# Closing layer norm of layer 1: beta joins the kept rows in the projections' stage, ACT normalises, and the gate's matmul has stationary weights

## The chip, the core and the metric

The kernel runs on one core of a Trainium2 chip. The metric is the time of the whole program on the device, in microseconds (us); lower is better. The engines named here are PE (TensorE), DVE (VectorE), ACT (ScalarE), POOL (GpSimd), and SP (SyncE), which issues most DMAs. Each runs its own list of instructions in order and waits for others on semaphores.

## The reference, cut to what matters

Four sequences of 1024 tokens (4096 rows of width 256) go through two layers. Layer 0 is windowed attention and a mixture of experts; layer 1 is full attention in groups, a layer norm with residual, and experts whose tokens are chosen with a Sinkhorn normalised gate. Only these lines bear on the change:

```python
# layer 1: attention on the normalised rows, _layernorm(x) is the block's input
out = ctx @ wo + bo
out = out + x                                   # x: the normalised input rows
mu, var = mean(out), var(out)
out = (out - mu) * rsqrt(var + 1e-5) * gamma + beta
# outer residual, then the next block's input norm and gate
x = x_before + out
y = _layernorm(x)                               # "routed rows"
gate_logits = einsum("bnd,de->bne", y, gate_w)  # 8 experts
```

So each row of `x_before` is needed again after attention, with `beta` added to it, and each new row is normalised once more, stored, and multiplied by a 256 x 8 gate.

## The kernel before, in words

The 4096 rows lie in SBUF as 32 tiles of 128 rows, `g.x[:, t, :]`, with `g.mean` and `g.rstd` beside them. Layer 1's first half is `attention1`, four stages one after the other with a barrier between them: `project_groups`, `group_attention`, `finish_stats`, `norm_residual`. Two of them are touched by the diff.

**Projections' stage (`project_groups`, names `pg_`).** There are 16 pairs of tiles, in 8 rounds of two (s = 0, 1). In a round DVE normalises 4 tiles into `pg_xn` (L1510), PE transposes them (L1579), ACT copies them out (L1546), PE makes queries and keys (L1590) and values (L1598), ACT writes the rounded part `pg_hi` (L1555), DVE the rest `pg_lo` (L1520) and the values `pg_v` (L1525), and SP stores all of it to DRAM. Beside this, x itself must be kept in DRAM and then be replaced in SBUF by `xn + bo`: SP stores the pair of tiles straight out of `g.x` (`keep_x`, L1434), POOL waits until that store has landed and adds `bo` (L1485). Between its first rounds POOL also sets six pieces of the key stack `a_ks` to one (L1493), two after each of the adds of rounds 0, 2 and 4. All is ordered by hand: DVE's loop is `rests(r, 0)`, `normalise(r + 1)`, `rests(r, 1)`; PE's is project, four transposes for each of two pairs, project; SP's is `keep(r, 0)`, `keep_x(r + 1)`, `keep(r, 1)`, and in rounds 1 to 4 six loads for the attention (L1382). `pg_hi` and `pg_lo` have one buffer for each s, so ACT and DVE may write those of round r + 1 only when the stores of round r have landed (`parts_out`).

**Closing stage (`norm_residual`, names `nr_`).** Eight steps of four tiles. SP loads gamma, beta, the kept rows `nr_xb` in four quarters and the gate. POOL adds beta to `nr_xb` (L1975, eight instructions of 128 x 1024). For each step DVE makes `(x - mean) * gamma` (L1986), then the new x (L1992), its statistics (L1997) and seven small operations (L2001 to L2011); ACT takes the root (L2036); DVE inverts it (L2015) and normalises the four tiles of the step before into `nr_xn` (L2021). SP stores these rows, PE transposes them (L2062), ACT copies them (L2042), PE multiplies with the transposed tile as the stationary operand and the 8 columns of the gate moving (L2068), and ACT copies the logits out (L2045). After the barrier comes `sinkhorn`, which needs all logits.

Of the kernel before, what the change touches and what calls it, by code (L numbers as in the profile page):

```python
# [1389 lines left out]
def project_groups(nc, g, parts, values, x_kept, qs, ks, v):  # L1390
# [4 lines left out]
    with phase(nc) as (e, semaphore, begin):  # L1395
# [13 lines left out]
        xn_ready, xnT_done, xnT_ready, qk_done, hi_ready, lo_ready, v_done, v_ready, xn_bo_ready = [sem(n) for n in (  # L1409
            "xn_ready", "xnT_done", "xnT_ready", "qk_done", "hi_ready", "lo_ready", "v_done", "v_ready", "xn_bo_ready")]  # L1410
# [4 lines left out]
        W_IN, B_IN, PARTS = 16 * 3, 16 * (2 * KD + A + 1), 16 * 4  # L1415

        @block.sync
        def _(sp):
# [8 lines left out]
            sp.dma_start(bo[:], ins["L1_attn_bo"].rearrange("(o n) -> o n", o=1).broadcast_to([P, D])).then_inc(b_in, 16)  # L1427
# [43 lines left out]
        def _(pool):  # L1471
# [5 lines left out]
            pool.wait_ge(b_in, ONE + B_IN)  # L1477

            def residual(r):
                for s in range(2):  # L1480
                    i = 2 * r + s
                    pool.wait_ge(x_out[s], ONE + 16 * r + 16)
                    for h in range(2):
                        pool.wait_ge(xn_ready, ONE + 2 * i + h + 1)
                        nc.gpsimd.tensor_tensor(g.x[:, bass.ds(2 * i + h, 1), :].rearrange("p o d -> p (o d)"),  # L1485
                                                xn[s][h][:], bo[:], ALU.add).then_inc(xn_bo_ready, 1)

            for a in range(SLOTS):
                residual(2 * a)
                pool.wait_ge(xn_bo_ready, ONE + 4 * (2 * a + 1))  # L1490
# [3 lines left out]
                pool.wait_ge(k_ones, ONE + 2 * (a + 1))  # L1494
                residual(2 * a + 1)
            with pool.Fori(2 * SLOTS, STEPS) as r:
                residual(r)

        @block.vector
        def _(dve):  # L1500
# [12 lines left out]

            def rests(r, s):
# [410 lines left out]
def norm_residual(nc, g, x_kept, gate, logits, rows_out):  # L1925
# [3 lines left out]
    C = 4  # L1929
    STEPS = T // C  # L1930
    QUARTERS = 4
    with phase(nc) as (e, semaphore, begin):
        sb = lambda n, shape, dt=F32: e.enter_context(nc.sbuf_tensor(f"nr_{n}", shape, dt))
        sem = lambda n: semaphore(f"nr_{n}")
        gamma, beta, eps = sb("gamma", [P, D]), sb("beta", [P, D]), sb("eps", [P, 1])
        xb = sb("xb", [P, T, D])
        gw = sb("gw", [P, KD, E])
        scaled = sb("scaled", [P, C, D])
        diff, var = sb("diff", [P, C]), sb("var", [P, C])
        xn = [sb(f"xn{s}", [P, D]) for s in range(C)]  # L1940
        xnT = [sb(f"xnT{s}", [P, KD, P]) for s in range(C)]
        w_in, gate_in, xb_ready, scaled_ready, x_ready, stats_ready, step, var_ready, std_ready, rstd_ready = [sem(n) for n in (
            "w_in", "gate_in", "xb_ready", "scaled_ready", "x_ready", "stats_ready", "step", "var_ready", "std_ready", "rstd_ready")]
        xn_ready, xnT_done, xnT_ready, l_done, l_ready = [sem(n) for n in (
            "xn_ready", "xnT_done", "xnT_ready", "l_done", "l_ready")]
        xb_in = [sem(f"xb_in{n}") for n in range(QUARTERS)]
        rows_kept = [sem(f"rows_kept{s}") for s in range(C)]
        block = begin()
        b_tp, b_l = g.bank[0:C], g.bank[C]
        four = lambda i: bass.ds(C * i, C)  # L1950

        @block.sync
        def _(sp):
# [453 lines left out]
```

## Time and profile before

| what | us |
|---|---|
| time, median of 3 runs | 2563.13 |
| lowest and highest of the 3 | 2553.75, 2564.44 |
| the profiled execution's own time | 2581.78 |
| its span in the trace | 2579.9 |
| PE, DVE, ACT, POOL busy | 2096.3, 1623.0, 1009.0, 453.7 |

The busy times are sums over the whole program; each stage has a bound of its own. The projections' stage lies at about 1338 to 1468 us of the span and the closing stage at about 2241 to 2338 us. How far a time in the trace is from the start of the span is what the first column of a timeline shows.

### The profile page before, as it was taken

Reading aid. Unit: us, or ns where it says so; the run is one execution under the profiler, and the core shown is the slowest. Engines: PE = TensorE matmul, PEld = TensorE weight load, DVE = VectorE, ACT = ScalarE, POOL = GpSimd, SP = SyncE. Lnnn points to the kernel's source line nnn. Section 1 sums busy time; section 2 is a strip of 40 time slices with the busy share of each in tenths; the row PEclk is TensorE's granted clock in tenths of the full one; section 3 lists DMA queues with packets and bytes.
Section 4 is the critical chain, followed back from the end, with each engine's and each line's share of the span. In section 5 each row is a group of like instructions: output and inputs, shape, how many; then the busy total and the mean of one; then the engine's idle time right before and its main releaser. Section 6 shows DMA issues by size and latency. Waiting matters only on the chain. (4 is left out here: it accounts for less than half of the span.)

```text
span 2579.9 us, 47888 instructions
## 1 busy us (share of the span) xinstructions
PE 2096.3 (81%) x16968; PEld 1310.4 (51%) x16969; DVE 1623.0 (63%) x2749; ACT 1009.0 (39%) x1885; POOL 453.7 (18%) x612
## 2 busy tenths in 40 slices
PE   2888888679799999996968899999999999643150
PEld 2666666368566666665857633333333333242140
DVE  4666666557443334334654599999999999286922
ACT  2545554332100000002322257777877778410010
POOL 3000000200111111102434111111111111110054
PEclk9999999889899999997989879999999999855585
DMA  2000000551211111113328888755754700210054
GB/s 82 2 0 0 0 0 0 196 221 66 79 41 41 41 41 41 41 37 126 110 73 272 230 60 71 60 46 46 64 37 41 61 2 2 70 49 16 1 162 131
DMA packets 207090, 171.36 MB, mean 66 GB/s; under 512 B 121772, under 2 KB 184920, under 8 KB 204920
## 3 DMA queue, kind: packets, MB, share of 16 engines
q1 hardware_dynamic: 186872, 126.57, 26.2%
q0 software_dynamic: 17792, 26.39, 3.8%
q10 hardware_dynamic: 2304, 16.78, 1.8%
q8 instruction: 76, 1.25, 0.2%
q14 instruction: 46, 0.38, 0.1%
HBM read 105.43 MB, written 63.97 MB: 66 GB/s over the span
## 5 line engine op out<-in xcount | busy, mean ns | idle before, releaser
L1760 DVE TENSOR_REDUCE ga_nmax<-banks 128x1 fp32r<-128x1024 f32 x512 | 620.7, 1220 | 47.1 <-PE banks L1836 45.5
L1791 ACT ACTIVATE ga_probT<-banks 128x512 f32<-128x512 f32 x1024 | 553.4, 598 | 180.3 <-PE banks L1849 133.8
L1836 PE MATMUL banks<-a_ks,a_qs 48*128 48x512 f32 x1024 | 378.6, 457 | 28.1 <-DVE ga_nmax L1760 22.8
L1849 PE MATMUL banks<-a_qs,a_ks 49*128 49x512 f32 x1024 | 375.6, 447 | 0.7 <-ACT ga_probT L1791 0.7
L1865 PE MATMUL banks<-ga_probT,a_v 128*32 128x256 f32 (+1 forms) x3840 | 320.4, 406 | 6.4 <-ACT ga_o L1797 6.4
L1836 PEld LDWEIGHTS banks<-a_ks,a_qs 48*128 48x128 f32 x1024 | 159.4, 193 | 238.1 <-DVE ga_nmax L1760 174.4
L1275 PE MATMUL banks<-m_w,rb_xT 128*128 x576 | 273.8, 598 | 0.0
L1748 POOL DMA_DIRECT2D a_qs<-ga_max_rows x256 | 130.8, 519 | 599.7 <-DVE ga_max_rows L1767 556.4
L1257 ACT ACTIVATE rb_silu<-banks 128x512 f32<-128x512 f32 x72 | 43.0, 597 | 435.0 <-PE banks L1275 435.0
L1088 PE MATMUL banks<-sh_xnT,sh_w 128*128 128x512 f32 x768 | 184.9, 399 | 32.0 <-DVE sh_w L874 30.9
L1088 PEld LDWEIGHTS banks<-sh_xnT,sh_w 128*128 128x128 f32 x768 | 146.4, 193 | 65.1 <-issue 34.9
L1849 PEld LDWEIGHTS banks<-a_qs,a_ks 49*128 49x128 f32 x1024 | 154.5, 186 | 24.8 <-ACT ga_probT L1791 21.8
L1865 PEld LDWEIGHTS banks<-ga_probT,a_v 128*32 128x32 f32 x3840 | 76.0, 108 | 179.1 <-ACT ga_probT L1791 129.5
L1275 PEld LDWEIGHTS banks<-m_w,rb_xT 128*128 128x128 f32 x576 | 110.3, 191 | 78.1 <-issue 70.6
L346 DVE TENSOR_REDUCE wa_nmax<-banks 128x4 f32<-128x512 f32 x128 | 87.0, 680 | 95.3 <-PE banks L543 95.3
L1195 POOL DMA_INDIRECT rb_xb<-normalised_rows,m_source x72 | 68.4, 950 | 385.9 <-PE banks L1268 385.4
L1302 PE MATMUL banks<-rb_w,rb_gluT 128*128 x576 | 135.9, 378 | 0.0
L414 ACT ACTIVATE wa_probT<-banks 128x512 f32<-128x512 f32 x128 | 76.4, 597 | 128.9 <-PE banks L555 128.9
L1228 DVE TENSOR_SCALAR rb_own_out<-rb_row_e,m_block_f 128x128 fp32r<-128x128 f32 x72 | 20.7, 287 | 151.1 <-PE banks L1292 151.1
L1302 PEld LDWEIGHTS banks<-rb_w,rb_gluT 128*128 128x128 f32 x576 | 104.1, 190 | 11.6 <-issue 0.2
L555 PE MATMUL banks<-ident,wa_prob 128*128 128x128 f32 x512 | 85.8, 291 | 25.7 <-ACT wa_prob L407 25.7
L407 ACT ACTIVATE wa_prob<-wa_ex 128x512 f32<-128x512 f32 x128 | 80.5, 629 | 51.9 <-DVE wa_ex L348 51.0
(297 smaller groups left out, 3256.6 us busy)
## 6 DMA issues: line engine op xcount, KB each, us to landing
sh_xnT<-xnT_parts ACTq DMA_DIRECT2D x16, 1024.0 KB, 4.9
sorted_out<-rb_yb SPq DMA_DIRECT2D x72, 128.0 KB, 1.7
xnT_parts<-np_parts SPq DMA_DIRECT2D x8, 1024.0 KB, 7.7
m_w<-in_L_ffn_rw_dram SPq DMA_DIRECT2D x2, 4096.0 KB
values<-pg_v SPq DMA_DIRECT2D x16, 512.0 KB, 3.1
a_v<-values SPq DMA_DIRECT2D x16, 512.0 KB, 9.0
a_qs<-queries_rounded SPq DMA_DIRECT2D x28, 256.0 KB, 8.8
a_ks<-keys_rounded SPq DMA_DIRECT2D x28, 256.0 KB, 10.1
```

The source lines that it names most:

```text
L346: nc.vector.tensor_reduce(nmax[k][:], sc, axis=AX.X, op=ALU.max, negate=True).then_inc(max_ready, 1)
L407: nc.scalar.activation(prob[k][:], ex[k][:], ACT.Exp, scale=SCALE).then_inc(prob_ready, 1)
L555: last = nc.tensor.transpose(b_pt[k][:, P * j:P * (j + 1)], prob[k][:, j, :], g.ident[:])
L1088: last = nc.tensor.matmul(bank[m % 2][:], w[a][:, k, P * m:P * (m + 1)], xnT[s][:, b, k, :], start=(k == 0 and a + b == 0), stop=(k == KD ...
L1275: last = nc.tensor.matmul(bank[:], xT[s][:, k, :], flat[:, bass.ds(n * KD + k, 1), :].rearrange("p o h -> p (o h)"), start=False, stop=(k ...
L1302: last = nc.tensor.matmul(b_y[:, 0:D], gluT[:, m, :], flat[:, bass.ds(n * KH + m, 1), :].rearrange("p o d -> p (o d)"), start=False, stop= ...
L1748: nc.gpsimd.dma_start(dst, src).then_inc(max_in[1][b % 2], 16)
L1760: nc.vector.tensor_reduce(nmax[b % 2][:, at:at + 1], slot[:], axis=AX.X, op=ALU.max, negate=True).then_inc(use_read, 1)
L1791: nc.scalar.activation(probT[k % SETS][2 * h + n][:], b_t[ring_place["weights", w] % RING][:], ACT.Exp, scale=SCALE).then_inc(exp_ready, 1)
L1836: return nc.tensor.matmul(slot[:, HALF * kh:HALF * (kh + 1)], qs[a][rows, n, P * q:P * (q + 1)], ks[a][rows, n, HALF * kh:HALF * (kh + 1)] ...
L1849: nc.tensor.matmul(bank[:], ks[a][rows, 2 * gp + n, P * kt:P * (kt + 1)], qs[a][rows, 2 * gp + n, HALF * hf:HALF * (hf + 1)], start=True, ...
L1865: last = nc.tensor.matmul(b_o[at:at + BL, cols], v[c % SLOTS][:, h, 2 * gp + n, kt, :], probT[k % SETS][2 * h + n][:, cols], start=(kt == ...
```

## The change

In the projections' stage beta is loaded too. DVE now writes `x + beta` of each pair into a new buffer `pg_kept` (one for each s), SP stores from that buffer, and DVE, not POOL, adds `bo`. These two are a new function `residual(r + 1)` at the end of DVE's loop body. `keep_x` waits for `kept_ready`. POOL has only its memsets left and no longer waits for adds between them.

In the closing stage the loop over steps is unrolled. POOL has no adds; it sets the gate's 128 x 256 tile to zero once. DVE no longer normalises; it stores the negated mean, and ACT normalises in two passes, `x + (-mean)` and then times `rstd`. The gate's weights, padded with zeros to 128 columns, are now the stationary operand, and 512 tokens move; the 128 x 512 result is copied by ACT (`nr_lT`), turned back by four transposes on PE, and then copied to the logits. PE and ACT work one and two steps behind the rows.

```diff
@@ project_groups
+        beta = sb("beta", [P, D])
+        kept = [sb(f"kept{s}", [P, 2, D]) for s in range(2)]
...
             def keep_x(r):
                 for s in range(2):
                     i = 2 * r + s
-                    sp.wait_ge(xn_bo_ready, ONE + 4 * r)
-                    sp.dma_start(x_dst[bass.ds(i, 1)].rearrange("i p s d -> (i p) s d"), g.x[:, bass.ds(2 * i, 2), :]).then_inc(x_out[s], 16)
+                    sp.wait_ge(kept_ready, ONE + i + 1)
+                    sp.dma_start(x_dst[bass.ds(i, 1)].rearrange("i p s d -> (i p) s d"), kept[s][:]).then_inc(x_out[s], 16)
...
@@ gpsimd
-            pool.wait_ge(b_in, ONE + B_IN)
...
+            pool.wait_ge(v_one, ONE + 2)
             for a in range(SLOTS):
-                residual(2 * a)
-                pool.wait_ge(xn_bo_ready, ONE + 4 * (2 * a + 1))
+                if a:
+                    pool.wait_ge(k_ones, ONE + 2 * a)
                 for h in range(2):
                     rows = slice(HR * h + BL, HR * h + HR)
                     nc.gpsimd.memset(ks[a][rows].bitcast(F32), 1.0).then_inc(k_ones, 1)
-                pool.wait_ge(k_ones, ONE + 2 * (a + 1))
-                residual(2 * a + 1)
-            with pool.Fori(2 * SLOTS, STEPS) as r:
-                residual(r)
@@ vector
+            def residual(r):
+                for s in range(2):
+                    i = 2 * r + s
+                    pair = g.x[:, bass.ds(2 * i, 2), :]
+                    dve.wait_ge(x_out[s], ONE + 16 * r)
+                    nc.vector.tensor_tensor(kept[s][:], pair, beta[:].unsqueeze(1).broadcast_to([P, 2, D]),
+                                            ALU.add).then_inc(kept_ready, 1)
+                    dve.wait_ge(kept_ready, ONE + i + 1)
+                    dve.wait_ge(xn_ready, ONE + 2 * i + 2)
+                    for h in range(2):
+                        nc.vector.tensor_tensor(g.x[:, bass.ds(2 * i + h, 1), :].rearrange("p o d -> p (o d)"),
+                                                xn[s][h][:], bo[:], ALU.add).then_inc(xn_bo_ready, 1)
...
             normalise(0)
+            residual(0)
             with dve.Fori(0, STEPS - 1) as r:
                 rests(r, 0)
                 normalise(r + 1)
                 rests(r, 1)
+                residual(r + 1)
@@ norm_residual, vector
             def inverse(i):
                 dve.wait_ge(std_ready, ONE + i + 1)
                 nc.vector.reciprocal(g.rstd[:, four(i)], g.rstd[:, four(i)]).then_inc(rstd_ready, 1)
-                dve.wait_ge(rstd_ready, ONE + i + 1)
...
-                    nc.vector.tensor_scalar(xn[s][:], tile(g.x, t), g.mean[:, bass.ds(t, 1)], g.rstd[:, bass.ds(t, 1)],
-                                            ALU.subtract, ALU.mult).then_inc(xn_ready, 1)
...
             new_x(0)
-            with dve.Fori(1, STEPS) as i:
+            for i in range(1, STEPS):
                 new_x(i)
-                normalise(i - 1)
-            normalise(STEPS - 1)
+                inverse(i - 1)
+            inverse(STEPS - 1)
@@ norm_residual, scalar
+                for c in range(C):
+                    t = C * i + c
+                    nc.scalar.activation(xn[i % 2][:, c, :], g.x[:, t, :], ACT.Identity,
+                                         bias=g.mean[:, t:t + 1]).then_inc(centred_ready, 1)
+                act.wait_ge(rstd_ready, ONE + i + 1)
+                for c in range(C):
+                    t = C * i + c
+                    act.wait_ge(centred_ready, ONE + t + 1)
+                    nc.scalar.activation(xn[i % 2][:, c, :], xn[i % 2][:, c, :], ACT.Copy,
+                                         scale=g.rstd[:, t:t + 1]).then_inc(xn_ready, 1)
...
+            for i in range(STEPS + 3):
+                if i < STEPS:
+                    root(i)
+                    normalised(i)
+                if 1 <= i <= STEPS:
+                    transposed(i - 1)
+                if 2 <= i <= STEPS + 1:
+                    gated(i - 2)
+                if i >= 3:
+                    kept(i - 3)
@@ norm_residual, tensor
+                for k in range(KD):
+                    last = nc.tensor.matmul(b_g[i % 2], gw[:, k, :], xnT[i % 2][:, k, :], start=(k == 0), stop=(k == KD - 1))
+                last.then_inc(gate_done, 1)
...
+            for i in range(STEPS + 2):
+                if i < STEPS:
+                    transposes(i)
+                if 1 <= i <= STEPS:
+                    gates(i - 1)
+                if i >= 2:
+                    turned(i - 2)
```

Three places in the order of instructions matter. The first is POOL's whole list in the projections' stage. Before, it was this (the names are those above; `ISA` and the like are waits and loop code):

```order
L1473 MEMSET pg_v 128x1024 x2
L1476 MEMSET pg_v 128x32 x2
L1485 TENSOR_TENSOR x<-pg_xn,pg_bo 128x256 x4
L1493 MEMSET a_ks 32x4096 x2
L1485 TENSOR_TENSOR x<-pg_xn,pg_bo 128x256 x8
L1493 MEMSET a_ks 32x4096 x2
L1485 TENSOR_TENSOR x<-pg_xn,pg_bo 128x256 x8
L1493 MEMSET a_ks 32x4096 x2
L1485 TENSOR_TENSOR x<-pg_xn,pg_bo 128x256 x4
```

Now it is this, with the barrier's and the stage's branch ahead of it and the jump behind:

```order
L77 UNCONDITIONAL_BRANCH
L1473 UNCONDITIONAL_BRANCH
L1476 MEMSET pg_v 128x1024 x2
L1479 MEMSET pg_v 128x32 x2
L1486 MEMSET a_ks 32x4096 x6
L64 UNCONDITIONAL_BRANCH
```

The adds are gone, and the six memsets of the key stack, which stood in three places, follow each other at the stage's start.

The second place is DVE at the start of the same stage, with the first part of its loop. Before:

```order
L1510 TENSOR_SCALAR pg_xn<-x,mean,rstd 128x256 x4
L1529 UNCONDITIONAL_BRANCH
L1529 ISA
L1519 ISA
L1520 SCALAR_TENSOR_TENSOR pg_lo<-banks,pg_b_qk,pg_hi 128x256 x2
```

And now:

```order
L1499 TENSOR_SCALAR pg_xn<-x,mean,rstd 128x256 x4
L1508 TENSOR_TENSOR pg_kept<-x,pg_beta 128x512
L1513 TENSOR_TENSOR x<-pg_xn,pg_bo 128x256 x2
L1508 TENSOR_TENSOR pg_kept<-x,pg_beta 128x512
L1513 TENSOR_TENSOR x<-pg_xn,pg_bo 128x256 x2
L1532 UNCONDITIONAL_BRANCH
L1532 ISA
L1521 ISA
L1522 SCALAR_TENSOR_TENSOR pg_lo<-banks,pg_b_qk,pg_hi 128x256 x2
```

Six additions stand between the last normalised tile and the first `pg_lo`; the same six stand at the end of each of the loop's seven turns.

The third place is the end of the closing stage on PE. There it ended with one more turn of the same loop, four times two transposes and 16 small products. Now its last rows are these, where `nr_xn` is transposed at L2089, the gate is applied at L2097 and the logits are turned at L2105:

```order
L2089 MATMUL banks<-ident,nr_xn 128x128 x8
L2097 MATMUL banks<-nr_xnT,nr_gw 128x512 x2
L2105 MATMUL banks<-ident,nr_lT 128x128 x4
L2097 MATMUL banks<-nr_xnT,nr_gw 128x512 x2
L2105 MATMUL banks<-ident,nr_lT 128x128 x8
```

Behind the last rows' transposes there are now two gates and twelve turning transposes, where one step's products stood before.

## Rows read from the trace of the kernel before

**Rows 1.** Timeline, closing stage's opening: start us, us, engine line op out<-in xcount [idle before <-releaser]

```profile
2249.97 19.14 POOL L1975 TENSOR_TENSOR nr_xb<-nr_xb,nr_beta 128x1024 f32 x8 [50.66 <-DMA nr_xb<-x_kept]
2252.34 9.98 DVE L1992 SCALAR_TENSOR_TENSOR x<-nr_scaled,rstd,nr_xb 128x256 f32<-128x256 f32 x4 [4.58 <-POOL nr_xb L1975]
```

**Rows 2.** Timeline, closing stage, a steady step and the end

```profile
2278.04 1.67 DVE L1986 SCALAR_TENSOR_TENSOR nr_scaled<-x,mean,nr_gamma 128x256 f32<-128x256 f32 x4
...
2281.68 1.41 DVE L1997 BATCH_NORM_STATS2 stats<-x  x4 [0.16 <-DVE x L1992]
...
2284.34 0.18 DVE L2015 RECIPROCAL rstd<-rstd  x1
...
2284.89 1.38 DVE L2021 TENSOR_SCALAR nr_xn<-x,mean,rstd 128x256 f32 x4 [0.37 <-DVE rstd L2015]
...
2286.32 1.67 DVE L1986 SCALAR_TENSOR_TENSOR nr_scaled<-x,mean,nr_gamma 128x256 f32<-128x256 f32 x4
...
2325.57 0.16 DVE L2011 TENSOR_SCALAR rstd<-nr_var 128x4 f32 x1
...
2326.81 1.96 PE L2062 MATMUL banks<-ident,nr_xn 128*128 128x128 f32 x8 [3.10 <-DVE nr_xn L2021]
...
2337.04 0.20 ACT L2045 ACTIVATE gate_logits<-banks 128x32 f32<-128x32 f32 x1 [2.83 <-PE banks L2068]
```

**Rows 3.** Stretches: us, busy (x) of PE, PEld, DVE, ACT, POOL, PEclk, DMA share, GB/s

```profile
2300.00:2330.00 30.00, 18.73 (x88) 18.46 (x88) 25.19 (x87) 7.91 (x23) 0.00 (x0) 0.50 0.20 70
```

**Rows 4.** Timeline, opening of the projections' stage

```profile
1340.36 0.21 POOL L1476 MEMSET pg_v<- 128x32 f32 x2
...
1343.33 0.62 SPq L1427 DMA_DIRECT2D pg_bo<-in_L_attn_bo_dram  x1
...
1346.81 1.80 DVE L1510 TENSOR_SCALAR pg_xn<-x,mean,rstd 128x256 f32<-128x256 f32 x4 [9.77 <-DMA pg_bo<-in_L_attn_bo_dram]
...
1349.57 2.81 PE L1590 MATMUL banks<-pg_xnT,pg_wq 128*128 128x256 f32 x8
...
1356.81 1.98 DVE L1510 TENSOR_SCALAR pg_xn<-x,mean,rstd 128x256 f32 x4
```

**Rows 5.** Timeline, later rounds of the projections' stage

```profile
1372.68 1.37 DVE L1510 TENSOR_SCALAR pg_xn<-x,mean,rstd 128x256 f32 x4
...
1383.19 0.88 DVE L1520 SCALAR_TENSOR_TENSOR pg_lo<-banks,pg_b_qk,pg_hi 128x256 fp32r<-128x256 f32 x2 [2.29 <-ACT pg_hi L1555]
...
1387.54 1.96 SPq L1434 DMA_DIRECT2D x_kept<-x  x2
...
1390.37 0.84 ACT L1555 ACTIVATE pg_hi<-banks,pg_b_qk 128x256 fp32r<-128x256 f32 x2 [1.71 <-PE banks L1590]
...
1408.73 7.06 POOL L1493 MEMSET a_ks<- 32x4096 f32 x2
...
1414.19 2.72 DVE L1510 TENSOR_SCALAR pg_xn<-x,mean,rstd 128x256 f32 x4
...
1430.75 1.37 DVE L1510 TENSOR_SCALAR pg_xn<-x,mean,rstd 128x256 f32 x4
```

**Rows 6.** Instructions on pg_xn: engine op xcount: ns min/median/max, starts, forms

```profile
L1510 DVE TENSOR_SCALAR pg_xn<-x,mean,rstd x32: 394/407/1760, 1346.8 to 1445.6; 128x256 f32 x28, 128x256 f32<-128x256 f32 x4
```

**Rows 7.** DMA issues, 1380 to 1405 us: KB each, median us to landing

```profile
keys_rest<-pg_lo SPq DMA_DIRECT2D x4, 256.0 KB, 3.0
```

**Rows 8.** Timeline, layer 0's stage with the gate in the same form

```profile
487.03 1.09 ACT L669 ACTIVATE np_xnT<-banks 128x512 f32<-128x512 f32 x2
...
487.32 1.88 PE L720 MATMUL banks<-np_xnT,np_gw 128*128 128x512 f32 x4
...
489.04 0.60 PE L728 MATMUL banks<-ident,np_lT 128*128 128x128 f32 x4
```

**Rows 9.** Groups by line and shape, ACT: busy us, mean ns, idle before

```profile
L1042 ACT ACTIVATE sh_p<-sh_p 128x256 f32<-128x256 f32 x1 | 0.4, 416 | 0.0
```

**Rows 10.** Groups by line, PE, 689 to 704 us

```profile
L1275 PE MATMUL banks<-m_w,rb_xT 128*128 x15 | 10.4, 832 | 0.0
```

More of the change, by code:

```diff
@@ L1942, in norm_residual @@
[L1942 to L1945, printed above, removed]
+        xn = [sb(f"xn{u}", [P, C, D]) for u in range(2)]
+        xnT = [sb(f"xnT{u}", [P, KD, C * P]) for u in range(2)]
@@ L1946, in norm_residual @@
         xb_in = [sem(f"xb_in{n}") for n in range(QUARTERS)]
-        rows_kept = [sem(f"rows_kept{s}") for s in range(C)]
+        rows_kept = [sem(f"rows_kept{u}") for u in range(2)]
         block = begin()
-        b_tp, b_l = g.bank[0:C], g.bank[C]
-        four = lambda i: bass.ds(C * i, C)
+        b_tp = [g.bank[2 * u:2 * u + 2] for u in range(2)]
+        b_g, b_l = g.bank[4:6], g.bank[6:8]
+        four = lambda i: slice(C * i, C * (i + 1))
+        half = lambda h: slice(TH * P * h, TH * P * (h + 1))
@@ L2048, in _, with normalised @@
-            root(0)
-            with act.Fori(1, STEPS) as i:
-                root(i)
-                transposed(i - 1)
-            transposed(STEPS - 1)
+            def normalised(i):
+                if i >= 2:
+                    act.wait_ge(xnT_done, ONE + HALVES * (i - 1))
+                    act.wait_ge(rows_kept[i % 2], ONE + 16 * (i // 2))
+                for c in range(C):
[8 more added lines that the diff above has]
+                                         scale=g.rstd[:, t:t + 1]).then_inc(xn_ready, 1)
@@ new lines, in transposed @@
+            def transposed(i):
+                for h in range(HALVES):
+                    act.wait_ge(xnT_done, ONE + HALVES * i + h + 1)
+                    if i >= 2 and h == 0:
+                        act.wait_ge(gate_done, ONE + i - 1)
+                    dst = xnT[i % 2][:, :, half(h)].rearrange("p k (t q) -> p t k q", t=TH)
+                    nc.scalar.activation(dst, b_tp[i % 2][h].rearrange("p (t k q) -> p t k q", t=TH, k=KD),
+                                         ACT.Copy).then_inc(xnT_ready, 1)
@@ new lines, in gated, with kept @@
+            def gated(i):
+                act.wait_ge(gate_done, ONE + i + 1)
+                if i >= 2:
+                    act.wait_ge(l_done, ONE + i - 1)
+                nc.scalar.activation(lT[i % 2][:], b_g[i % 2], ACT.Copy).then_inc(lT_ready, 1)
+            def kept(i):
+                act.wait_ge(l_done, ONE + i + 1)
+                src = b_l[i % 2].rearrange("p (c q) -> p c q", c=C)[:, :, 0:E]
+                nc.scalar.activation(logits[:, four(i), :], src, ACT.Copy).then_inc(l_ready, 1)
@@ new lines, in transposes @@
+            def transposes(i):
+                for h in range(HALVES):
+                    if i >= 2:
+                        pe.wait_ge(xnT_ready, ONE + HALVES * (i - 2) + h + 1)
+                    for c in range(TH):
+                        t = TH * h + c
+                        pe.wait_ge(xn_ready, ONE + C * i + t + 1)
+                        for k in range(KD):
+                            at = P * (KD * c + k)
+                            last = nc.tensor.transpose(b_tp[i % 2][h][:, at:at + P], xn[i % 2][:, t, P * k:P * (k + 1)], g.ident[:])
+                    last.then_inc(xnT_done, 1)
```

117 lines of the change are left out of this document (49 added, 68 removed).

## The prediction, made before the changed kernel ran

> **What bounds the kernel now.** I began with the page's busy times only to see that no engine is busy throughout, so each stage is read by itself. The timeline of the closing stage came next, because most of the change is there. Its opening shows DVE waiting for POOL: POOL starts its eight additions when the first quarter of the kept rows is in, at 2249.97, and holds on for 19.14 us; DVE's first four additions to x, which take 0.42 us each later, take 9.98 together [rows 1]. One POOL addition takes 19.14/8 = 2.39 us, one of DVE's 9.98/4 = 2.50: each DVE instruction waits for one POOL instruction to end. Afterwards DVE bounds the stage: from the first instruction of a step to that of the next is 2286.32 - 2278.04 = 8.28 us, with idle time of only 0.16 and 0.37 us in the rows [rows 2]. PE works in about five eighths of a stretch there, at a granted clock of 0.50, the lower level [rows 3], and it waited 3.10 us for DVE's rows [rows 2]. The last statistics are done at 2325.73, and the last logits leave at 2337.24, 11.5 us later [rows 2].
>
> In the projections' stage the reader should see a loop of PE, ACT and DVE in which nobody is full: an undisturbed round takes (1414.19 - 1372.68)/3 = 13.84 us, and DVE has a hole of 2.29 us in it [rows 5]. No semaphore makes DVE late for POOL there, and yet POOL holds it up: the four normalised tiles at 1414.19 took 2.72 us and not 1.37, beside a memset pair of 7.06 us that ends at 1415.79 [rows 5]; one of these instructions took 1760 ns where the median is 407 [rows 6]. 1414.19 + 1.76 is 1415.95, just after the memset's end. The round after it took 1430.75 - 1414.19 = 16.56 us, 2.7 more than its neighbours [rows 5].
>
> **The closing stage, part by part.** *Opening.* Without POOL's additions DVE adds as soon as the first quarter has landed. Its load is issued one DMA earlier, so 2249.5 (2249.97 less some 0.4). A step from its second group to the inversion is 8.28 less what comes before and after: 2284.34 - 2278.04 = 6.30, less 1.67 + 0.15 for the scaling, which is done by then, less 0.16 for a wait that is now taken instruction by instruction: 4.3 us. The first statistics are ready at 2253.8 to 2254.3. The memset of the gate's tile costs nothing: it runs while DVE waits for loads.
>
> *Steps.* DVE loses the normalising (1.38), the idle time before it (0.37), the hand-over (0.05) and the two grouped waits (0.15 and 0.16): 8.28 - 2.11 = 6.17 us. Seven steps are 43.2, so the last statistics are done at about 2297.5, where they were done at 2325.73: 28.2 us earlier.
>
> *Is DVE still the bound?* ACT's step: eight passes over 128x256 at 0.416, the only row with source and result in SBUF [rows 9], though two with a bias from PSUM take 0.84 together [rows 5], so 3.3; two halves 1.09, the 512 wide logits 0.6 [rows 8], a root of at most 0.4 and the logits' copy 0.20 [rows 2]: 5.6 us, below 6.17. PE's step at the upper clock, as in layer 0's stage: transposes 1.1 to 1.3, gate 1.88, turning 0.60 [rows 8], about 3.5. At the lower clock: 1.96 for eight transposes [rows 2], four products at 0.832 [rows 10] = 3.3, half of 1.96 for the turning: 6.2 to 6.4. So the step is 6.17 to 6.4; I take 6.17 and keep 7 x 0.2 = 1.4 us for the range.
>
> The Trainium skill ("ScalarE: Activation LUTs", Rules for kernel authors) speaks against this part: additions and products belong on VectorE, and an ACTIVATE with a bias read from memory costs about 0.3 us and 0.83 ns an element. By that eight passes would be 4.1 us, an estimate from that page, and ACT's step 6.4; the row of 0.416 us lies below it.
>
> *End.* After the last statistics (T) ACT still has to scale step 6 (1.7), copy and turn over older steps (2.0), take the root, centre and scale step 7 (3.7): rows complete at T + 7.5. PE then has transposes, gate of step 6, turning of step 5, gate of step 7, turning of 6 and 7. At the upper clock this is about 1.3 + 1.9 + 0.5 + 1.7 + 0.5, then the turning of step 7 behind ACT's copy of 0.6: logits at T + 14. At the lower clock PE is late already from step 5: 7.5 + 1.7 + 3.4 + 1 + 3.4 + 1 + 1 = T + 19. Before it was T + 11.5. The stage's rows say lower clock [rows 3], the stage with this same PE work ran at the upper one's speeds [rows 8]; with both near, I take T + 17, 5.5 us later than before. The stage gains 28.2 - 5.5 = 22.7 us, with bounds of 20 and 26.
>
> **The projections' stage.** *Gone:* POOL's memset no longer meets the normalising of round 5: 2.7 us of the 16.56 [rows 5]. The one beside round 1 cost (1.98 - 1.37) = 0.6 [rows 4], and that round too was long, 1372.68 - 1356.81 = 15.87 against 13.84. I count up to 1.4 of it as PE's slower start after the longer pause.
>
> *New:* the six memsets now start when POOL's small ones end, at 1340.57 [rows 4], and 7.06/2 = 3.53 us each puts their ends at 1344.1, 1347.7, 1351.2, 1354.7, 1358.3 and 1361.8. DVE starts when the last of its weights is in, one DMA later than 1346.81: bo was issued at 1343.33 [rows 4], beta follows some 0.65 later, so 1347.4. The first tile then gets in at 1347.7. Each further tile waits for one memset, if what POOL's additions did in the closing stage [rows 1] holds here: tiles at 1351.2, 1354.7 and 1358.3. PE has both pairs' transposes ahead of its first project (at 1349.57 before) [rows 4], so project starts at about 1359.9, 10.3 us late (the second pair's transposes and PE's start take 1.1 after 1358.7). If DVE comes only after 1347.7, everything moves by one more memset: 13.8. The transposed copies, `pg_hi` and `pg_lo` queue behind it unchanged.
>
> The six additions of `residual(0)` wait for no one else's data and end before `pg_hi` comes. The Trainium skill ("SBUF — State Buffer", Who interferes with whom) says that an instruction with two SBUF inputs meets only a POOL instruction that reads SBUF, so a memset would not stop them; no row of this trace shows such a pair. By the other reading the last memset holds the first of them and adds 0.5 us.
>
> *Loop:* `residual` is two additions of 128x512 and four of 128x256. DVE's passes over 256 columns are 1.41/4 = 0.35 to 1.67/4 = 0.42 apart [rows 2], so these are 8 x 0.35 to 8 x 0.42 = 2.8 to 3.4, with the wait on its own result in each half some 3.0 us, into DVE's hole of 2.29 us before `pg_lo` [rows 5]. The first `pg_lo` slips by 0.7, and the pause before the values' addition takes it up: 0 to 0.1 us a round. The row of no such addition stands in this stage; if the six took 3.6 and not 3.0, a round would move by 0.4 at most, and if 2.3, by nothing.
>
> *SP:* this is the new wait. `keep_x` stands ahead of `keep(r, 1)`, and was issued 1 us after the tiles (1387.54, where the tiles are due at 1372.68 + 13.84 = 1386.52) [rows 5]. Now it waits for DVE's second `pg_kept`, about 10.4 us after the tiles. Behind it queue five stores of `keep(r, 1)`, in four rounds six loads, and `keep(r + 1, 0)`. From tiles at 1372.68: kept at 1383.1, its stores issued by 1385, the four parts by 1387, landed 3.0 to 3.6 later [rows 7] at 1390 to 1390.6; ACT writes that buffer again at 1390.37 [rows 5]. So there is nothing left to spare. I take 1.5 us in all, with ends of 0 and 6.
>
> Sum for this stage: +10.3 (or 13.8), -0.6 and -1.4 in round 1, -2.7 in round 5, +1.5: +7 to +10.6. I take +8.5.
>
> **Sum.** -22.7 + 8.5 = -14.2 us against the profiled execution's 2581.78 (span 2579.9 and some 2 around it), or -0.55%. Of the median 2563.13 that is 14.1: 2549 us.
>
> **Rivals.**
> 1. *The memsets don't hold DVE one by one.* DVE issues 1.4 us of tiles and gets through between them or beside them. For it: the median of 32 instructions is undisturbed [rows 6], and the waits seen are all at the last memset of a pair. Against it: rows 1. Then the projections' stage gains 2 to 3.5 and the total is -26: 2537 us.
> 2. *POOL keeps the lock through all six.* DVE's first tile comes at 1361.8, project at 1364.3, +14.7; the rest as before: -22.7 + 11.5 = -11, or 2552 us. Near the forecast and within its range.
> 3. *ACT becomes the bound of the closing stage.* Two passes for every tile, waits between the passes and the copies for PE: if ACT's step is 8.3, as DVE's was, only the opening's gain is left, 28.2 - 7 x 2.1 = 13.4, less 6.5 for the end: -7, and with +8.5 the total is about +1: 2565 us. Against it: 5.6 us from the rows; the passes would have to cost 0.75 each.
> 4. *Slower: SP's queue closes a loop.* `pg_kept`, `keep_x`, the stores, their landing, `pg_hi`, `pg_lo`, `pg_kept` again: 0.9 + 2.0 + 3.6 + 6.5 = 13.0 of a round of 13.84. It decides once landing takes over 4.4 us in the bunched queue. At 7 us each of seven rounds is 2.6 longer, with PE falling to the lower clock in longer pauses 1.4 more: +28, and with the memsets +36: total +14, 2577 us. The landing of 3.0 [rows 7] is from spread stores; DMAs are busy there already.
>
> **Chances.** Forecast 0.50; rival 1 0.19; rival 2 0.12; rival 3 0.09; rival 4 0.10, half of it in a mild form near 2556. The range of 2534 to 2567 reaches from rival 1 with the upper clock at the end to rival 3. Less than 0.5% (12.8 us) can't be told from no change here. The forecast's own band, 2542 to 2556, has that bound, 2550, inside it: faster 0.3 + 0.19 + 0.05 = 0.54; same 0.2 + 0.07 + 0.08 + 0.03 = 0.38; slower 0.08.
>
> **What would show it.** DVE's `pg_xn` tiles at the start: four with about 3.5 us between them, and PE's first product near 1360. Rounds of 13.84 with no idle time of ACT or DVE on `parts_out`. In the closing stage DVE steps of 6.2 us without idle time, the first x at 2249.5 of that stage's old position, and 14 to 19 us from the last statistics to the last logits. It is wrong if DVE waits for ACT's roots in each step, or if the rounds are longer than 14.

## The result and the profile after

The kernel before took 2558.44 us (median of 4 runs, the three shown above and one of 2545.54) and the changed one 2528.59 us (4 runs, 2521.94 to 2529.55). The ratio is 0.9884, with a 95% interval of 0.9839 to 0.993: 18 to 41 us faster. The forecast was 2549 us with a range of 2534 to 2567, so the time lies below the range.

| stage, us | before | after | forecast change | measured |
|---|---|---|---|---|
| projections, to the attention's first work | 130.1 | 140.3 | +8.5 (+7 to +10.6) | +10.2 |
| closing stage, to the first row of `sinkhorn` | 96.7 | 65.2 | -22.7 (-20 to -26) | -31.5 |
| the untouched last stage, from the first `re_taken` on PE | 113.4 | 83.8 | 0 | -29.6 |
| everything else | 2239.7 | 2230.9 | 0 | -8.8 |
| span | 2579.9 | 2520.2 | | -59.7 |

The two profiled executions differ by 59.7 us and the medians by only 29.9. The third row of the table is therefore suspect, and the experiments take it up first. "Everything else" lies between 2230.9 and 2247.4 us in all 13 traces, whichever kernel ran, so its -8.8 us is within what it varies by.

The closing stage's opening after the change, on a timeline (start, us, instruction, idle time and what ended it), answers to [rows 1]:

```profile
2244.51 0.35 SPq L1962 DMA_DIRECT2D nr_gamma<-in_L_attn_gamma_dram  x1
...
2248.92 1.67 DVE L1985 SCALAR_TENSOR_TENSOR nr_scaled<-x,mean,nr_gamma 128x256 f32<-128x256 f32 x4 [4.27 <-DMA nr_gamma<-in_L_attn_gamma_dram]
2252.74 1.67 DVE L1993 SCALAR_TENSOR_TENSOR x<-nr_scaled,rstd,nr_xb 128x256 f32<-128x256 f32 x4 [2.15 <-DMA nr_xb<-x_kept]
...
2256.58 0.16 DVE L2012 TENSOR_SCALAR rstd<-nr_var 128x4 f32<-128x4 f32 x1
```

POOL is gone from it. Four of DVE's x take 1.67 us, where four took 9.98 beside POOL's additions, and only the load of the kept rows is waited for. The first statistics are done at 2256.74, which is 12.2 us after the stage's start at 2244.51.

A steady step and the end, answering to [rows 2]:

```profile
2290.00 1.64 DVE L1985 SCALAR_TENSOR_TENSOR nr_scaled<-x,mean,nr_gamma 128x256 f32<-128x256 f32 x4
2290.12 1.71 ACT L2044 ACTIVATE nr_xn<-nr_xn,rstd 128x256 f32<-128x256 f32 x4 [0.54 <-DVE rstd L2016]
...
2293.14 1.40 DVE L1998 BATCH_NORM_STATS2 stats<-x 128x6 f32<-128x256 f32 x4
...
2293.43 1.70 ACT L2038 ACTIVATE nr_xn<-x,mean 128x256 f32<-128x256 f32 x4
...
2295.40 0.16 DVE L2012 TENSOR_SCALAR rstd<-nr_var 128x4 f32<-128x4 f32 x1
2295.47 0.17 DVE L2016 RECIPROCAL rstd<-rstd 128x4 f32<-128x4 f32 x1
...
2300.58 1.70 ACT L2044 ACTIVATE nr_xn<-nr_xn,rstd 128x256 f32<-128x256 f32 x4
...
2303.29 1.98 PE L2097 MATMUL banks<-nr_xnT,nr_gw 128*128 128x512 f32 x4 [0.52 <-ACT nr_xnT L2053]
...
2305.55 1.88 PE L2097 MATMUL banks<-nr_xnT,nr_gw 128*128 128x512 f32 x4
...
2308.81 0.20 ACT L2065 ACTIVATE gate_logits<-banks 128x32 f32<-128x32 f32 x1 [0.66 <-PE banks L2105]
```

The step before began with its scaling at 2284.45, so a step is 5.55 us. DVE has no idle time in it, and ACT waits 0.54 us for DVE's inversion: DVE is the bound, as forecast. The last statistics are done at T = 2295.56, 51.1 us after the stage's start, and the last logits at 2309.01, or T + 13.5.

The same stage in a stretch (us, busy and count of PE, PEld, DVE, ACT, POOL, granted clock, DMA share, GB/s), answering to [rows 3]:

```profile
2262.00:2292.00 30.00, 19.86 (x75) 10.65 (x76) 29.31 (x109) 24.79 (x63) 0.00 (x0) 0.82 0.26 88
```

DVE is busy for 29.31 of 30 us, where it was 25.19, and the granted clock rose from 0.50 to 0.82, so PE was mostly at 2.4 GHz and no longer at 1.2.

The projections' stage's opening, answering to [rows 4]:

```profile
1333.14 1.84 POOL L1476 MEMSET pg_v<- 128x1024 f32 x2 [16.29 <-POOLq L77]
...
1335.31 21.46 POOL L1486 MEMSET a_ks<- 32x4096 f32 x6
...
1342.07 11.24 DVE L1499 TENSOR_SCALAR pg_xn<-x,mean,rstd 128x256 f32<-128x256 f32 x4 [10.36 <-DMA pg_beta<-in_L_attn_beta_dram]
...
1353.94 0.76 DVE L1513 TENSOR_TENSOR x<-pg_xn,pg_bo 128x256 f32<-128x256 f32 x2
...
1354.28 3.62 PE L1594 MATMUL banks<-pg_xnT,pg_wq 128*128 128x256 f32 x8
...
1362.44 1.37 DVE L1499 TENSOR_SCALAR pg_xn<-x,mean,rstd 128x256 f32 x4
```

The six memsets run from 1335.31 to 1356.77. Four tiles that take 1.37 us alone take 11.24 among them: the first passes in 0.45 us, and each of the other three takes 3.67 to 3.68, beside memsets of 3.50 to 3.55 us. PE's first product comes 21.1 us after the stage's start at 1333.14, where it came after 11.1.

### The profile page after: what moved, and what is told of

Read it like the earlier page. It is cut to its first block and busy times, and to the rows that moved or that the text cites. A ratio compares the mean times of both kernels' runs of the same rounds, so it can differ in the third digit from the quotient of the medians.

```text
span 2520.2 us, 47264 instructions
## 1 busy us (share of the span) xinstructions
PE 2078.8 (82%) x16904; PEld 1280.2 (51%) x16905; DVE 1623.2 (64%) x2765; ACT 1033.4 (41%) x1941; POOL 414.5 (16%) x573
## 5 line engine op out<-in xcount | busy, mean ns | idle before, releaser
L346 DVE TENSOR_REDUCE wa_nmax<-banks 128x4 f32<-128x512 f32 x128 | 86.9, 679 | 96.7 <-PE banks L543 96.7
L414 ACT ACTIVATE wa_probT<-banks 128x512 f32<-128x512 f32 x128 | 76.5, 598 | 129.9 <-PE banks L555 129.9
```

Source lines behind the costliest of these rows:

```text
L346: nc.vector.tensor_reduce(nmax[k][:], sc, axis=AX.X, op=ALU.max, negate=True).then_inc(max_ready, 1)
```

## Experiments

The runs come in three groups, e1 to e4, e5 to e8 and e9 to e11. Each group ran on one chip at one time and shared its runs of the kernel before. Stage lengths are read from the traces as in the table above (P the projections' stage, C the closing one, L the last).

| run | this, before (medians) | ratio, 95% | P | C | L |
|---|---|---|---|---|---|
| e1 | 2579.01, 2576.34 | 0.9992, 0.9971 to 1.0013 | 129.0 | 96.7 | 109.7 |
| e2 | 2544.78, 2576.34 | 0.9866, 0.9834 to 0.9899 | 129.9 | 65.0 | 111.0 |
| e3 | 2568.72, 2576.34 | 0.9975, 0.9955 to 0.9995 | 140.5 | 80.8 | 110.0 |
| e4 | 2568.80, 2576.34 | 0.9966, 0.994 to 0.9993 | 130.0 | 89.8 | 107.7 |
| e5 | 2532.57, 2553.77 | 0.9903, 0.9865 to 0.9941 | 139.9 | 65.3 | 84.7 |
| e6 | 2512.76, 2553.77 | 0.9841, 0.9811 to 0.9872 | 126.4 | 65.0 | 84.0 |
| e7 | 2534.33, 2553.77 | 0.9922, 0.9896 to 0.9948 | 140.8 | 73.4 | 84.8 |
| e8 | 2534.07, 2553.77 | 0.9928, 0.9905 to 0.9951 | 140.1 | 66.8 | 87.7 |
| e9 | 2522.35, 2550.03 | 0.99, 0.987 to 0.993 | 136.6 | 65.1 | 84.4 |
| e10 | 2523.78, 2550.03 | 0.9899, 0.9873 to 0.9925 | 136.4 | 65.8 | 83.5 |
| e11 | 2550.39, 2550.03 | 1.001, 0.9988 to 1.0033 | 130.1 | 96.7 | 85.0 |

### The last stage: e1, e5, e11

No edit: e1 and e11 are the kernel before, e5 is the changed one.

> The kernel before, profiled once more. The trace of the change is 59.7 us shorter in its span (2579.9 to 2520.2) where the medians differ by 29.9. Theory A: 24 us or more of that is the last stage (experts, not touched) of one execution of before, 241.9 us from the start of sinkhorn to the end against 210.5 after; then this run's last part is within 5 us of 212 and its span near 2556. Rival: the old closing stage leaves something behind that makes the untouched last stage longer (rows written in smaller DMAs); then it is 235 or more again and the span 2575 or more.

> The changed kernel, profiled once more. From the start of sinkhorn to PE's first work on chosen tokens and on to the end, no line is touched, yet the last 84 us in its first trace are 108 to 113 in all five other traces. Theory: those 84 us belong to that execution or its chip; here the last part is 105 us or more, the closing stage 65 and the projections' stage 140 again, and the span about 2551. Rival: the changed kernel leaves the last stage faster (rows stored in larger DMAs); then it is 90 or less and the late memsets' 111 us are what is odd.

> The kernel before, unchanged, beside the other two. Theory A (the 24 us by which the untouched last stage was shorter in the changed kernel's first trace belong to the chip of a call and not to the kernel): the last stage takes the same here as in the two other traces of this call, within 3 us, 84 to 88 us if this call's median of before is near 2554 and 108 to 113 us if it is near 2576. Theory B (the old kernel leaves the last stage long): 108 to 113 us here and 84 to 88 us in the two others.

The span of e1 was 2575.5 and not near 2556, and e5's last stage took 84.7 us, so the first two guesses of where the last stage's 30 us belong missed. The table shows that it isn't the kernel: all four kernels of the first group, old and new, have 107.7 to 111.0; all seven of the other two groups, which ran on two other chips, have 83.5 to 87.7, and e11 is the old kernel with 85.0. The stage's length goes with the group, that is with the chip or with the time at which it ran; each chip was used only once, so the runs don't separate these two. Its products of PE, by busy time, mean and idle time, first in the trace before, then in e11:

```profile
L2309 PE MATMUL banks<-re_w,re_takenT 128*128 128x256 f32 x128 | 36.7, 414 | 10.3 <-issue 5.2 <-ACT re_takenT L2334 3.2 <-DVE re_y L2347 1.8
```

```profile
L2309 PE MATMUL banks<-re_w,re_takenT 128*128 128x256 f32 x128 | 35.4, 403 | 1.6 <-ACT re_takenT L2334 1.1 <-DVE re_y L2347 0.3
```

The work is nearly equal (36.7 and 35.4 us); the idle time, half of it with nothing that the profile shows as waited for, is 10.3 against 1.6. That is 8.7 of the 28.4 us between the two stages. The same 16.28 MB moved at a mean of 144 GB/s in the trace before and at 194 in e11. Why stays open. For the change it means that the net of the two stages, -31.5 + 10.2 = -21.3 us, is what the profiles show, and e5 against its own chip's runs measured 2532.57 - 2553.77 = -21.2, with an interval of -15 to -34.

### What the closing stage's gain is made of: e3, e4, e7, e8

e3 has the new projections' stage and the old closing stage without POOL's additions (the loads of beta and all waits stay, beta is in the kept rows):

```diff
@@ norm_residual, gpsimd (old closing stage)
-                with pool.Fori(n * STEPS // QUARTERS, (n + 1) * STEPS // QUARTERS) as i:
-                    nc.gpsimd.tensor_tensor(xb[:, four(i), :], ..., ALU.add).then_inc(xb_ready, 1)
+                pool.sem_inc(xb_ready, STEPS // QUARTERS)
```

> The projections' stage as changed, the closing stage as before but without POOL's additions (beta is in the kept rows already; POOL only passes the arrival of each quarter on). Theory: the closing stage loses its opening only, from 96.7 to about 81 us, steps stay at 8.28 us; the projections' stage stays at 140. So the program is about 5 us below before (-15.5 + 10.2): the end of POOL's additions alone is worth half of the closing stage's 31.5. Rival: steps get shorter too without POOL at work, to below 8.0; then the closing stage is at 78 or less.

Its first x and two steps on DVE:

```profile
2257.97 1.67 DVE L1993 SCALAR_TENSOR_TENSOR x<-nr_scaled,rstd,nr_xb 128x256 f32<-128x256 f32 x4 [1.92 <-POOLq L1977]
...
2278.81 1.67 DVE L1987 SCALAR_TENSOR_TENSOR nr_scaled<-x,mean,nr_gamma 128x256 f32<-128x256 f32 x4
...
2287.08 1.67 DVE L1987 SCALAR_TENSOR_TENSOR nr_scaled<-x,mean,nr_gamma 128x256 f32<-128x256 f32 x4
```

The stage falls from 96.7 to 80.8 with steps still at 8.28. So POOL's additions alone cost 15.9 us, all of it at the opening. They slowed no steady step, since in the kernel before they ended at 2269.11 [rows 1], ahead of the second step.

e4 is the kernel before with nothing but DVE's loop of the closing stage unrolled, so that addresses are constants and not computed from a register:

```diff
@@ norm_residual, vector (old closing stage)
-            tile = lambda a, t: a[:, bass.ds(t, 1), :].rearrange("p o d -> p (o d)")
+            tile = lambda a, t: a[:, t, :]
...
-            with dve.Fori(1, STEPS) as i:
+            for i in range(1, STEPS):
```

> The kernel before with one edit: DVE's loop over the closing stage's steps is written out, so that no address comes from a register; same operations, same grouped waits, POOL's additions kept. The changed kernel's step is 5.55 us where 6.17 was forecast. Theory: the missing 0.6 us a step is the loop's register work between DVE's instructions, so the step here is 7.7 us and not 8.28 and the closing stage 4 us shorter, 92.5. Rival: it is the waits taken instruction by instruction; then the step stays at 8.2 to 8.3.

One step in e4:

```profile
2277.12 1.67 DVE L1987 SCALAR_TENSOR_TENSOR nr_scaled<-x,mean,nr_gamma 128x256 f32<-128x256 f32 x4
2278.89 1.67 DVE L1993 SCALAR_TENSOR_TENSOR x<-nr_scaled,rstd,nr_xb 128x256 f32<-128x256 f32 x4
2280.60 1.41 DVE L1998 BATCH_NORM_STATS2 stats<-x 128x6 f32<-128x256 f32 x4
...
2282.93 0.17 DVE L2016 RECIPROCAL rstd<-rstd 128x4 f32<-128x4 f32 x1
2283.14 1.38 DVE L2022 TENSOR_SCALAR nr_xn<-x,mean,rstd 128x256 f32<-128x256 f32 x4
2284.44 1.67 DVE L1987 SCALAR_TENSOR_TENSOR nr_scaled<-x,mean,nr_gamma 128x256 f32<-128x256 f32 x4
```

The step is 7.31 to 7.32 us, 0.97 less than 8.28 where 0.6 was expected, with every instruction as long as before. Against [rows 2] the time went from between them: scaling to statistics 3.64 and now 3.48, statistics to inversion 2.66 and now 2.33, inversion to normalising 0.55 and now 0.21, normalising to scaling 1.43 and now 1.30. Over seven steps that is the stage's 6.9 us. The trace before has register instructions (`FUSED_REGOPS`) of 46 to 99 ns on DVE's queue at each group of passes in such a step; e4 has none there. Their share is not separated from that of the loop itself.

e7 is the changed kernel with the normalising back on DVE:

```diff
@@ norm_residual
+                for c in range(C):   # DVE, behind its inversion
+                    nc.vector.tensor_scalar(xn[i % 2][:, c, :], g.x[:, t, :], g.mean[:, t:t + 1], g.rstd[:, t:t + 1], ALU.add, ALU.mult).then_inc(xn_ready, 1)
...
-                    normalised(i)   # ACT
```

> The changed kernel, but DVE makes nr_xn in one pass after the inversion as before, and ACT's eight passes a step are gone. Theory: the step is DVE's 5.55 us and 1.38 more, with the wait for the inversion 7.1 to 7.3 us; seven steps are 11 to 12 us longer. The end is shorter, since ACT's chain of centring and scaling goes: from 13.5 us after the last statistics to about 11. The closing stage is 74 us against 65.2. So moving the pass to ACT is worth 9 us of the 31.5. Rival: ACT in the changed kernel is nearly the bound (it waited 0.54 us a step), so the step falls to DVE's 6.9 and only 7 us are lost.

Two of its steps:

```profile
2274.31 1.67 DVE L1985 SCALAR_TENSOR_TENSOR nr_scaled<-x,mean,nr_gamma 128x256 f32<-128x256 f32 x4
2280.01 1.38 DVE L2023 TENSOR_SCALAR nr_xn<-x,mean,rstd 128x256 f32<-128x256 f32 x4
2281.31 1.67 DVE L1985 SCALAR_TENSOR_TENSOR nr_scaled<-x,mean,nr_gamma 128x256 f32<-128x256 f32 x4
```

The step is 7.00 and the stage 73.4, so moving the normalising to ACT is worth 8.1 us, between the 9 expected and the rival's 7. That closes the account: 15.9 (POOL's additions), 7.4 (from e3's 80.8 to e7's 73.4: the unrolling, and every other edit of the stage) and 8.1 make 31.4 of 31.5.

e8 is the changed kernel with the gate's old form, the transposed tile stationary and 8 columns moving, and no turning back:

```diff
@@ norm_residual, tensor
-                for k in range(KD):
-                    last = nc.tensor.matmul(b_g[i % 2], gw[:, k, :], xnT[i % 2][:, k, :], ...)
+                for c in range(C):
+                    for k in range(KD):
+                        last = nc.tensor.matmul(b_l[i % 2][:, E * c:E * (c + 1)], xnT[i % 2][:, k, P * c:P * (c + 1)], gw[:, k, 0:E], ...)
```

> The changed kernel with the gate's product as before: the transposed tile is stationary, 8 columns move, no turning and no copy of 512 columns. Theory: DVE bounds the steps either way, so they stay at 5.55 us; PE needs 3.5 us a step for it at the lower clock and has room. The end gets shorter by about one stage of the pipeline (gate, copy, turning, copy: 1.9 + 0.6 + 0.6 + 0.2 against 3.5 + 0.2): the closing stage is 63 to 67 us. So the gate's form is worth nothing within 2 us. Rival: the wide product is what raises PE's clock; without it PE stays at the lower level, its step of 5.4 to 5.6 us becomes the bound and the stage is 70 or more.

PE in two of its steps:

```profile
2296.87 1.94 PE L2087 MATMUL banks<-ident,nr_xn 128*128 128x128 f32 x8
2298.94 3.58 PE L2096 MATMUL banks<-nr_gw,nr_xnT 128*128 128x8 f32 x16
2302.43 1.94 PE L2087 MATMUL banks<-ident,nr_xn 128*128 128x128 f32 x8
```

PE spends 1.94 + 3.58 = 5.52 of a step of 5.56 us. It just fits, and DVE stays the bound: ACT waits 1.03 us for it in each step. The same kernel in a stretch, columns as above:

```profile
2272.00:2302.00 30.00, 26.73 (x119) 23.93 (x119) 28.91 (x111) 22.79 (x60) 0.00 (x0) 0.50 0.29 95
```

The half of the rival that speaks of the clock came true: with the gate's old form PE stays at 0.50, the lower level, in steps as short as those with 0.82 above. With the new form and the longer steps of e7 it had 0.73 from 2280 to 2310 us. The other half did not, since PE's work fits into the step even so. The stage is 66.8 us, so the new form of the gate is worth 1.5. All of it lies at the end, where the last logits come at T + 15.1 and not at T + 13.5; the expectation had the end shorter with the old form, so its 63 to 67 us was met without its reason.

### What the projections' stage's loss is made of: e2, e6, e9, e10

e2 puts the memsets late: each pair waits until DVE's tiles of its round are done. e10 turns SP's order alone, and e6 has both edits:

```diff
@@ project_groups, gpsimd (e2, e6)
             for a in range(SLOTS):
+                pool.wait_ge(xn_ready, ONE + 4 * (2 * a + 1))
@@ project_groups, sync (e6, e10)
-                keep_x(r + 1)
                 keep(r, 1)
+                keep_x(r + 1)
```

> The changed kernel, but POOL's pair of key memsets for slot a waits until DVE has normalised the tiles of round 2a, as they stood before in effect. Theory: six memsets in a row hold DVE's four first tiles, one each, so the projections' stage is 10.2 us longer than before (140.3 to 130.1); with them late the tiles take 1.4 us together and the stage falls to 127 to 130 us, the program to about 12 us below the changed kernel, 2517. Rival: the wait for beta and the stores behind pg_kept are what costs; then the stage stays within 3 us of 140.

> The changed kernel with SP's order turned: keep(r, 1) stands ahead of keep_x(r + 1) in the projections' stage; the six early memsets stay. Theory A (ACT's waits for keys_rest, 10.8 us in five waits, come from the five stores that stand behind keep_x): these waits are gone, and the projections' stage falls from 140.2 to 134 to 137 us, that is by about the 3.5 us which the same turn gave on top of the late memsets. Theory B (the waits come from the length of the landing itself): ACT still waits for keys_rest, and the stage stays at 139 to 141 us.

> Memsets late as in the run before this, and SP stores pg_kept behind the other five stores of a round, not ahead of them. Theory: with keep_x ahead, ACT waits 8.0 us in three places for the landing of keys_rest, 4.9 of it in the last round, where pg_hi is written sooner than in others; with the order turned these waits go and the stage falls from 129.9 to about 125.5 us. DVE's wait for x_out is not reached, since a round lies between. Rival: DMA throughput holds the last stores up whatever their order; then the stage stays at 129 or more.

The opening of e2:

```profile
1340.57 1.38 DVE L1500 TENSOR_SCALAR pg_xn<-x,mean,rstd 128x256 f32<-128x256 f32 x4 [10.37 <-DMA pg_beta<-in_L_attn_beta_dram]
...
1342.07 7.06 POOL L1487 MEMSET a_ks<- 32x4096 f32 x2 [8.34 <-DVE pg_xn L1500]
...
1342.58 0.76 DVE L1514 TENSOR_TENSOR x<-pg_xn,pg_bo 128x256 f32<-128x256 f32 x2
```

The tiles take 1.38 us again and the stage 129.9, 10.4 less. The residual's additions run their usual 0.76 in the midst of a memset that began 0.5 us before.

ACT's waits for a store in the changed kernel, four of 1.4 to 1.5 us and this one, in the last round; under it the same place in e10:

```profile
1441.16 0.84 ACT L1559 ACTIVATE pg_hi<-banks,pg_b_qk 128x256 fp32r<-128x256 f32 x2 [1.41 <-DMA keys_rest<-pg_lo]
...
1458.50 1.99 PE L1594 MATMUL banks<-pg_xnT,pg_wq 128*128 128x256 f32 x8
...
1462.51 1.57 ACT L1559 ACTIVATE pg_hi<-banks,pg_b_qk 128x256 fp32r<-128x256 f32 x4 [5.01 <-DMA keys_rest<-pg_lo]
...
1473.42 0.82 SPq L1382 DMA_DIRECT2D a_qs<-queries_rounded  x2
```

```profile
1446.15 0.84 ACT L1559 ACTIVATE pg_hi<-banks,pg_b_qk 128x256 fp32r<-128x256 f32 x2 [1.41 <-PE banks L1594]
...
1463.49 1.99 PE L1594 MATMUL banks<-pg_xnT,pg_wq 128*128 128x256 f32 x8
...
1465.52 0.84 ACT L1559 ACTIVATE pg_hi<-banks,pg_b_qk 128x256 fp32r<-128x256 f32 x2 [3.03 <-PE banks L1594]
...
1474.43 0.82 SPq L1382 DMA_DIRECT2D a_qs<-queries_rounded  x2
```

The short waits cost nothing: in e10 ACT sits idle for the same 1.41 us, for PE, and rounds are 13.84 us in both. Only the last round pays. From PE's last `pg_wq` to the attention's first load it is 14.92 us in the changed kernel and 10.94 in e10, 4.0 less, as the stages say (140.3 and 136.4). e6 has both gains, 126.4, and is faster than either kernel: 0.9841 of before on its chip, where the changed kernel had 0.9903. Their intervals overlap a little (0.9872 and 0.9865 are the inner ends), but the two stages show 13.8 us between them.

e9 is the changed kernel with each memset cut in four of 32x1024:

```diff
@@ project_groups, gpsimd
-                    nc.gpsimd.memset(ks[a][rows].bitcast(F32), 1.0).then_inc(k_ones, 1)
+                    for q in range(4):
+                        part = nc.gpsimd.memset(ks[a][rows, NG // 4 * q:NG // 4 * (q + 1)].bitcast(F32), 1.0)
+                    part.then_inc(k_ones, 1)
```

> Each of the six memsets of the key stack at the projections' stage's start is cut into four of 32x1024, about 0.9 us each; nothing else differs from the changed kernel. Theory A (a tile of DVE's waits for whichever memset holds the two engines' common SBUF access, one per tile): the four first tiles take about 1.0 us each, 3.6 to 4 us together instead of 11.24, PE's first projection comes near the stage's start plus 14, and the projections' stage falls from 140.2 to 132 to 134 us. Theory B (POOL keeps the access through all that it has queued, or a tile waits for a number of pieces that adds up to the same bytes): the first tiles stay 10 to 11 us or come all at the end of POOL's list, and the stage stays at 139 to 144 us.

```profile
1335.62 22.75 POOL L1487 MEMSET a_ks<- 32x1024 f32 x24
...
1342.39 3.77 DVE L1501 TENSOR_SCALAR pg_xn<-x,mean,rstd 128x256 f32<-128x256 f32 x4 [10.37 <-DMA pg_beta<-in_L_attn_beta_dram]
...
1347.13 3.62 PE L1596 MATMUL banks<-pg_xnT,pg_wq 128*128 128x256 f32 x8
...
1356.00 2.84 DVE L1501 TENSOR_SCALAR pg_xn<-x,mean,rstd 128x256 f32 x4
```

The four tiles take 3.77 us, the last three of them at most 1.12 each beside pieces of 0.95, as theory A had it, and theory B is out: what is lost goes by the length of one memset and not by POOL's queue. But the stage fell by 3.6 and not by 6 to 8: the size was missed. The first product came 7.5 us earlier, and then the second round's tiles (2.84 for 1.37) met POOL's last pieces and PE was slower there, so that round took 16.98 instead of 13.84: 3.1 given back, and 0.7 in the first round.

## Why the forecast was wrong

**Closing stage, the step that failed.** "8.28 - 2.11 = 6.17 us": the step is 5.55, and 7 x 0.62 = 4.3 us of gain were missed. The prediction took out the instructions that go and the idle times that a row named, and kept the rest at the rolled loop's length. From scaling to statistics it had 3.33 us and 3.14 were measured, from statistics to inversion 2.66 and 2.33, from inversion to the next scaling 0.18 and 0.09. e4 shows what it left in: unrolling alone takes 0.97 us a step from between instructions of unchanged length. Of these, 0.34 lay between inversion and normalising, which the sum had taken out already; the other three, 0.16 + 0.33 + 0.13, are the 0.62 that it kept. The diff said that the loop is unrolled, and no term of the sum priced it. The bounds of 20 to 26 had the same hole, since both ends used 6.17 or more.

**The end.** "I take T + 17" between 14 at the upper clock and 19 at the lower; it was T + 13.5, 3.5 us less. The prediction leant half on the old stage's clock of 0.50, but that clock belonged to the old form of the gate. In steps of the same 5.55 us PE had 0.82 with the new form and 0.50 with the old one (e8), and its last gates took 1.98 and 1.88 us, as in layer 0's stage [rows 8]. The opening gave another 0.8: first statistics 12.2 us after the stage's start, where the prediction's 2254.3 is 13.0. Together 4.3 + 3.5 + 0.8 = 8.6 of the 8.8 us missed.

**Is DVE still the bound?** Right. A pass of ACT lasts 0.50 us and not 0.416, but they overlap and four take 1.70, as in the sum. The rows of `nr_xn` (ns least, median, most):

```profile
L2038 ACT ACTIVATE nr_xn<-x,mean x32: 492/502/513, 2257.0 to 2300.2; 128x256 f32<-128x256 f32 x32
L2044 ACT ACTIVATE nr_xn<-nr_xn,rstd x32: 492/494/509, 2262.3 to 2301.8; 128x256 f32<-128x256 f32 x32
```

Rival 3 is out. The figure of the Trainium skill ("ScalarE: Activation LUTs", Rules for kernel authors), 0.3 us and 0.83 ns an element, gives 0.51 us for one such pass, and the trace agrees with 0.50. Adding it up eight times to 4.1 us, as the prediction did, overstates: the passes overlap, and eight took 3.4. Its advice to do additions and products on VectorE would have cost 8.1 us here (e7), because VectorE was the bound.

**Projections' stage, the memsets.** Right in kind and size. The forecast was one tile for one memset, with the first tile let in at once, and a first product 10.3 us late; it was 10.0 late, with up to 3.68 us for a tile. Rival 1 (they pass undisturbed) and rival 2 (POOL keeps the lock through all six) are both out, by the 11.24 us of four tiles while POOL went on for 3.5 us more, and by e9. The additions of `residual(0)` ran at 0.76 and 0.67 us before the last memset ended, no longer than in later rounds. The Trainium skill ("SBUF — State Buffer", Who interferes with whom) says that an instruction with two SBUF inputs meets a POOL instruction that reads SBUF and not one that only writes it; the trace agrees, and e2 shows the same. The lost rounds came back as forecast: round 1 fell from 15.87 to 13.84 us, round 5 from 16.56 to 13.84.

**SP's queue.** Found, and too small: 1.5 us (0 to 6) forecast, 4.0 measured (e10). It isn't a loop over seven rounds, as rival 4 had it. A round has slack for the late landing. The last has less, since PE has no next tiles to transpose between its two products: in e10 they start 5.57 us apart (1457.92 and 1463.49) and those of the round before 8.34 (1444.03 and 1452.37), so `pg_hi` is wanted 2.8 us sooner, and no later round takes the delay up. PE's first round took the other 0.9: the granted clock was 0.50 during its first 3.60 us, where the kernel before had 0.70 in its first 2.80. So 10.0 - 4.75 + 0.9 + 4.0 = +10.2.

**From the stages to the time.** The stages give -21.3 us and e5 -21.2; the first comparison gave -29.9 with an interval of 18 to 41. From the old median of 2563.13 the stages alone make 2541.8, which lies in the forecast's range, so the failed step and the end alone would not have carried the time out of it. The missed 8.8 less 1.7 in the projections' stage is 7.1 of the 20.4 us between 2549 and 2528.6; 4.7 are the old kernel's own median, which is 2558.44 with its fourth run; the remaining 8.6 are in no stage and within the measurement's interval. No run separates them further.

## What to carry to other kernels

When a loop is unrolled, price the unrolling. Subtract the time that the instructions themselves take from the step in the row of before, and what is left between them (here about 1 us of 8.3) is at stake. A step moved to an earlier stage takes its collisions with it: memsets of 3.5 us each, at the head of a stage, made three of the other engine's first four tiles as long as themselves, and set behind those tiles they cost nothing that shows (e2). A queue that is late by less than a round's slack costs nothing until the last round, which can have less, so price its delay there. Before two profiles are subtracted from each other, compare a stage that no edit touches: here such a stage differed by 29.6 us.

## What the runs showed of the hardware

- DVE's tiles get in between back-to-back memsets of POOL, one for each, as the prediction had it: a tile took up to 3.68 us among memsets of 3.54, and up to 1.12 among memsets of 0.95 (e9).
- The additions of POOL that cost 15.9 us met only the opening (e3). In the kernel before, DVE's four additions to x took 9.98 us beside them and two of its seven small operations 2.30 and 2.26 us for 0.16, while its four statistics instructions, which read one operand, took their usual 1.41.
- The granted clock followed the form of the gate's product: in steps of 5.55 and 5.56 us it was 0.82 with the new form and 0.50 with the old one, though PE was busy for 26.73 of 30 us in the latter (e8).
- The same program's last stage took 85.0 us on one chip and 109.7 on another, with nearly equal busy time (41.8 and 40.2 us of PE; e1, e11). The first profile of each kernel, with 113.4 and 83.8 us in that stage, showed a gain of 59.7 us for a change whose two stages bring 21.
